# Attention and output projection in one block of the program, with values copied by ScalarE, the sums' inverses spread by TensorE, and head loops written out

## What is computed

```python
q = jnp.einsum('btc,hcd->bhtd', x, Wq) + bq[None, :, None, :]
k = jnp.einsum('btc,hcd->bhtd', x, Wk) + bk[None, :, None, :]
v = jnp.einsum('btc,hcd->bhtd', x, Wv) + bv[None, :, None, :]
scores = jnp.einsum('bhtd,bhsd->bhts', q, k) * scale
neg = jnp.finfo(scores.dtype).min
causal = jnp.triu(jnp.full((Tn, Tn), neg, dtype=scores.dtype), k=1)
probs = jax.nn.softmax(scores + causal, axis=-1)
y = jnp.einsum('bhts,bhsd->bhtd', probs, v)
y = y.transpose(0, 2, 1, 3).reshape(Bn, Tn, H * D)
return y @ Wo + bo
```

## Time and profile before

| what | us |
|---|---|
| median of 3 runs | 2577.18 (2575.45 to 2577.74) |
| profiled execution, its own time | 2575.64 |
| its span, first to last instruction | 2574.1 |
| first row product of attention | at 182.3 |
| last product of the heads ends | at 624.3 |
| first product of the output projection | at 646.9 |
| last one starts | at 698.9 |

### The profile page before, as it was taken

The page is one execution under the profiler, slowest core; times in us unless marked ns, Lnnn a source line. Parts: engine busy times, 40 slices in busy tenths (PEclk is TensorE's granted clock), DMA queues, the critical chain, the costliest instruction groups (busy, mean ns, idle before and its releaser), DMA issues. The chain is left out here.

```text
span 2574.1 us, 47582 instructions
## 1 busy us (share of the span) xinstructions
PE 2334.5 (91%) x12710; PEld 1773.7 (69%) x12712; DVE 1497.5 (58%) x3155; ACT 977.3 (38%) x2202; POOL 1094.5 (43%) x993
## 2 busy tenths in 40 slices
PE   7969998996756999999999779999989998999998
PEld 5855455443535989989989648888855664788886
DVE  6336556663566555555555457999256665655554
ACT  3114555453254444444444342222255553312221
POOL 3128888776002666666667501111166663000000
PEclk9978999998866999999999879999999999999999
DMA  5458999996355999999999834447499761000001
GB/s 178 122 175 311 346 338 329 341 326 252 116 204 145 245 283 281 258 265 273 271 263 221 149 129 148 168 163 232 141 217 225 166 151 38 13 25 25 25 9 66
DMA packets 263307, 491.18 MB, mean 191 GB/s; under 512 B 31889, under 2 KB 149137, under 8 KB 253458
## 3 DMA queue, kind: packets, MB, share of 16 engines
q1 hardware_dynamic: 197202, 272.17, 34.9%
q0 software_dynamic: 62976, 212.42, 29.4%
q10 hardware_dynamic: 3024, 5.29, 0.6%
HBM read 592.96 MB, written 198.79 MB: 308 GB/s over the span
## 5 line engine op out<-in xcount | busy, mean ns | idle before, releaser
L1431 PE MATMUL m_ps_u<-m_ring,m_xT_hi 128*128 x1280 | 370.4, 350 | 0.2 <-issue 0.2
L1399 POOL DMA_INDIRECT expert_sum<-x_res,token_of x160 | 257.1, 1607 | 182.9 <-DMA expert_sum<-x_res,token_of 66.3
L808 ACT ACTIVATE probs<-ps_c 128x512 f32<-128x512 f32 (+3 forms) x384 | 179.1, 491 | 208.7 <-PE ps_c L741 102.7
L1431 PEld LDWEIGHTS m_ps_u<-m_ring,m_xT_hi 128*128 128x128 f32 x1280 | 236.7, 190 | 1.2 <-issue 0.6
L1431 PE MATMUL m_ps_u<-m_ring,m_xT_lo 128*128 x640 | 216.9, 339 | 0.0
L1392 POOL DMA_INDIRECT m_xg<-x_rows,token_of x160 | 172.5, 1078 | 100.6 <-issue 92.3
L709 PE MATMUL ps_r<-k_st,q_st 96*128 96x512 f32 (+3 forms) x384 | 163.8, 433 | 53.4 <-DVE neg_max L838 22.4
L1878 PE MATMUL s_ps<-s_x_hi,s_w_hi 128*128 128x512 f32 x512 | 199.7, 390 | 1.6 <-POOL s_w_lo L1848 1.6
L1878 PE MATMUL s_ps<-s_x_lo,s_w_hi 128*128 128x512 f32 x512 | 199.3, 389 | 0.0
L1878 PE MATMUL s_ps<-s_x_hi,s_w_lo 128*128 128x512 f32 x512 | 199.2, 389 | 0.0
L2647 DVE TENSOR_TENSOR x_res<-f_ps_o,x_res 128x512 f32<-128x512 f32 x176 | 109.3, 684 | 143.4 <-PE f_ps_o L2540 143.4
(11 more groups left out here) (357 smaller groups left out, 5782.0 us busy)
## 6 DMA issues: line engine op xcount, KB each, us to landing
m_ring<-w_split SPq DMA_DIRECT2D x160, 1536.0 KB
m_ring<-w_split SPq DMA_DIRECT2D x160, 768.0 KB
w_split<-e_gu_parts POOLq DMA_DIRECT2D x32, 1536.0 KB
proj<-s_out SPq DMA_DIRECT2D x32, 1024.0 KB, 4.0
e_raw_gu<-w_experts POOLq DMA_DIRECT2D x32, 768.0 KB
w_split<-e_dn_parts POOLq DMA_DIRECT2D x32, 768.0 KB
e_raw_dn<-w_experts POOLq DMA_DIRECT2D x32, 512.0 KB
q_st<-q_parts SPq DMA_DIRECT2D x32, 256.0 KB
```

The source lines that it names most:

```text
L808: nc.scalar.activation(probs[a][j % RING][:, :width], ps_c[(j * BATCH + a) % BUFS][:, :width], ACT.Exp, scale=SCALE).then_inc(exp_done, 1)
L1399: pool.indirect_dma_start(acc[j % 2], rows_at(j), y[j % TURNS], None, bounds_check=PADDED - 1, oob_is_err=True, compute_op=ALU.add).then_i ...
L1431: last = nc.tensor.matmul(ps_u[b % 2][:, :W_UP], x[b % 2][:, k, :], ring[:, first + k * GU_ROW:][:, bass.ds(place, W_UP)], start=(n == 0), ...
```

## The change

- `attend` and `output_projection` are put into one block: no wait of all engines between them. The output projection's tiles come from space that the heads don't use, and GpSimd's splitting of experts may go on beside it. The split of `wo` is in two halves, each behind and ahead of GpSimd's loop.
- The loops over heads on PE, ACT, DVE and SP are written out; GpSimd keeps its loop.
- `take_v` moves from GpSimd to ACT, behind the exponentials of column 5.
- q and k lie in device memory so that a half of both batches is one piece of 4 KB per row. `q_st` has three buffers, and a whole unit's q is loaded three units ahead, at the start of a unit. `y_st` is stored in halves, each with its own semaphore.
- In `parts` three small DVE operations (add, copy, subtract) become four small reductions.
- The inverses no longer go through device memory. `of_head` holds ones where a column belongs to a head, `of_chunk` the inverses of one group with zeros elsewhere; a 32-bit product of them on PE writes the spread inverses to PSUM (`o_ps_n`), DVE multiplies y into it, and ACT and DVE take the parts from there. y has 4 buffers of one step, the spread inverses 3, the output tiles 5.

```diff
@@ attention @@
-    qk = {n: nc.dram_tensor(f"{n}_parts", (HEADS, 2, DH, N_TOK), F32).ap() for n in "qk"}
+    qk = {n: nc.dram_tensor(f"{n}_parts", (HEADS, 2, DH, 2, BATCH, GROUP), F32).ap() for n in "qk"}
...
-        attend(nc, qk, v_rows, yT, all_sums, w_raw, w_split, wo, wo_hi, wo_lo)
-        output_projection(nc, x_res, yT, all_sums, inv_sums, wo_hi, wo_lo)
+        sb = lambda n, s, dt=F32: ctx.enter_context(nc.sbuf_tensor(n, s, dt))
+        wo_hi, wo_lo = sb("wo_hi", [P, KD, D], F32R), sb("wo_lo", [P, KD, D], F32R)
...
+        sem = semaphores(ctx, nc)
+        block = ctx.enter_context(nc.Block())
+        wo_split = sem("wo_split")
+        attend(nc, block, sem, qk, v_rows, yT, all_sums, w_raw, w_split, raw, parts, wo, wo_hi, wo_lo, wo_split)
+        output_projection(nc, block, sem, x_res, ident, yT, all_sums, wo_hi, wo_lo, wo_split, in_chunk, in_head, of_head)
@@ norm_and_project, home() @@
-            return qk["qk"[m // (MT // 2)]][h0:h0 + HT, part, :, g * GROUP:(g + 1) * GROUP]
+            return qk["qk"[m // (MT // 2)]][h0:h0 + HT, part, :, g % 2, g // 2, :]
@@ attend, GpSimd @@
-            def take_v(it, e):
-                u = unit(it, e)
-                if not (isinstance(it, int) and it == 0):
-                    pool.wait_ge(pv_done, (u - 1) * PER_UNIT + BATCH * RING)
-                    pool.sem_inc(turns_begun, 1)
-                nc.gpsimd.tensor_copy(v_pair[e][:, :, :DH], v_rows[:, :, bass.ds(u * DH, DH)]).then_inc(v_ready, 1)
...
+            def split_wo(half):
+                ks = slice(half * KD // 2, (half + 1) * KD // 2)
+                pool.wait_ge(wo_loaded, half * 16 + 16)
+                pool.sem_inc(turns_begun, 1)
+                nc.gpsimd.tensor_copy(wo_hi[:, ks, :], raw_wo[:, :, :]).then_inc(wo_split, 1)
+                pool.wait_ge(wo_split, half * 2 + 1)
+                pool.sem_inc(turns_begun, 1)
+                nc.gpsimd.tensor_tensor(wo_lo[:, ks, :], raw_wo[:, :, :], wo_hi[:, ks, :].bitcast(F32), ALU.subtract).then_inc(wo_split, 1)
...
             body(0, False)
+            split_wo(0)
             with pool.Fori(1, BODIES - 1) as it:
                 body(it, False)
+            split_wo(1)
             body(BODIES - 1, True)
...
@@ attend, SP @@
...
+            def store_y(u, half):
+                sp.wait_ge(y_done, u * 2 + half + 2)
+                cols = slice(half * HALF, (half + 1) * HALF)
                 for a in range(BATCH):
-                    toks = slice(a * T, (a + 1) * T)
-                    sp.dma_start(yT[bass.ds(u, 1), :, toks].rearrange("h d t -> (h d) t"), y_st[a * COL:a * COL + DH, :]).then_inc(y_stored, 16)
-                    sp.dma_start(all_sums[bass.ds(u, 1), toks], y_st[a * COL + DH:a * COL + DH + 1, :]).then_inc(y_stored, 16)
-
-            def body(it, final):
-                for e in range(E):
-                    if not final:
-                        after_column(it, e, 3)
-                        load_q(it + 1, e, 0, low_loaded[e])
-                        after_column(it, e, 7)
-                        load_k(it + 1, e, 0, low_loaded[e])
-                        after_column(it, e, NCH - 1)
-                        load_q(it + 1, e, 1, q_up_loaded[e])
-                        load_k(it + 1, e, 1, k_up_loaded[e])
-                    store(it, e)
-
...
+                    toks = slice(a * T + half * HALF, a * T + (half + 1) * HALF)
+                    sp.dma_start(yT[u:u + 1, :, toks].rearrange("h d t -> (h d) t"), y_st[a * COL:a * COL + DH, cols]).then_inc(y_stored[half], 16)
+                    sp.dma_start(all_sums[u:u + 1, toks], y_st[a * COL + DH:a * COL + DH + 1, cols]).then_inc(y_stored[half], 16)
...
+            for u in range(HEADS):
+                if u == 1:
+                    sp.wait_ge(wo_split, 2)
+                    load_wo(1)
+                if u + E < HEADS:
+                    sp.wait_ge(cols_done, u * PER_UNIT + 8 * BATCH)
+                    load_k(u + E, 0)
+                store_y(u, 0)
+                if u + E < HEADS:
+                    sp.wait_ge(cols_done, (u + 1) * PER_UNIT)
+                    load_k(u + E, 1)
+                store_y(u, 1)
+                if u + Q_BUFS < HEADS:
+                    for half in range(2):
+                        load_q(u + Q_BUFS, half)
@@ attend, TensorE and ScalarE @@
-            body(0, True, False)
-            with pe.Fori(1, BODIES - 1) as it:
-                body(it, False, False)
-            body(BODIES - 1, False, True)
+            for it in range(BODIES):
+                body(it, it == 0, it == BODIES - 1)
...
+            def take_v(u):
+                if u >= E:
+                    act.wait_ge(pv_done, (u - 1) * PER_UNIT + BATCH * RING)
+                nc.scalar.copy(v_pair[u % E][:, :, :DH], v_rows[:, :, u * DH:(u + 1) * DH]).then_inc(v_ready, 1)
...
+                        if j == 5 and E <= unit(it, e) + 1 < HEADS:
+                            take_v(unit(it, e) + 1)
@@ attend, VectorE @@
-                    nc.vector.tensor_tensor(blocks, blocks, second[:, :, :], ALU.min).then_inc(joined, 1)
+                    nc.vector.tensor_reduce(pairs[:, :, :, 0], both_max[:, :, :, :], AX.X, ALU.min).then_inc(joined, 1)
                     dve.wait_ge(joined, u + 1)
                 if not (isinstance(it, int) and it == 0 and e == 0 and half == 0):
                     dve.wait_ge(turned, u * 2 + half)
-                nc.vector.tensor_copy(of_batch[:, :, :, 0], blocks).then_inc(parts_done, 1)
-                dve.wait_ge(parts_done, u * 4 + half * 2 + 1)
-                nc.vector.tensor_tensor(of_batch[:, :, :, 1], blocks, of_batch[:, :, :, 0].bitcast(F32), ALU.subtract).then_inc(parts_done, 1)
+                nc.vector.tensor_reduce(pairs[:, :, :, 1].bitcast(F32R), pairs[:, :, :, 0:1], AX.X, ALU.max, negate=True).then_inc(parts_done, 1)
+                nc.vector.tensor_reduce(of_batch[:, :, :, 0], pairs[:, :, :, 0:1], AX.X, ALU.max).then_inc(parts_done, 1)
+                dve.wait_ge(parts_done, u * 6 + half * 3 + 2)
+                with nc.allow_low_precision(reason="one difference, rounded once to the type that the products read"):
+                    nc.vector.tensor_reduce(of_batch[:, :, :, 1], pairs, AX.X, ALU.add).then_inc(parts_done, 1)
...
-                if half == 0:
-                    dve.wait_ge(y_stored, (u + 1) * 64)
+                dve.wait_ge(y_stored[half], (u + 1) * 64)
@@ output_projection @@
+            sp.dma_start(sums[:, :], all_sums.rearrange("h (a t) -> (h a) t", t=W_SUMS)).then_inc(sums_loaded, 16)
+            for n, (g, k) in enumerate(STEPS):
+                if n >= Y_BUFS:
+                    sp.wait_ge(y_ready, n - Y_BUFS + 1)
+                heads = yT[k * HT:(k + 1) * HT, :, g * GROUP:(g + 1) * GROUP].rearrange("h d t -> (h d) t")
+                sp.dma_start(y[n % Y_BUFS][:, :], heads).then_inc(loaded[n % Y_BUFS], 16)
...
+            def spread_inverse(n):
+                g, k = STEPS[n]
+                if n >= BUFS:
+                    pe.wait_ge(lo_done, n - BUFS + 1)
+                if k == 0:
+                    pe.wait_ge(chunk_taken, (g + 1) * PER_GROUP)
+                nc.tensor.matmul(ps_n[n % BUFS][:, :], of_head[:, k * P:(k + 1) * P], of_chunk[g % 2][:, :, :].rearrange("p c t -> p (c t)"),
+                                 start=True, stop=True).then_inc(spread, 1)
...
+            pe.wait_ge(rows_marked, 3)
+            for n in range(BUFS):
+                spread_inverse(n)
+            pe.wait_ge(wo_split, 4)
+            for n in range(len(STEPS)):
+                pe.wait_ge(lo_done, n + 1)
                 for s in range(SUB):
...
+                    project_tile(n, s)
+                if n + BUFS < len(STEPS):
+                    spread_inverse(n + BUFS)
...
+            def take_chunks(g):
+                if g >= 2:
+                    act.wait_ge(spread, (g - 1) * KD)
+                for c in range(PER_GROUP):
+                    nc.scalar.activation(of_chunk[g % 2][:, c, :], sums[:, :], ACT.Copy, scale=in_chunk[:, g * PER_GROUP + c:g * PER_GROUP + c + 1]).then_inc(chunk_taken, 1)
...
+                dve.wait_ge(loaded[n % Y_BUFS], 16 * (n // Y_BUFS + 1))
+                dve.wait_ge(spread, n + 1)
+                nc.vector.tensor_tensor(ps_n[n % BUFS][:, :], y[n % Y_BUFS][:, :], ps_n[n % BUFS][:, :], ALU.mult).then_inc(y_ready, 1)
```

More of the change, by code:

```diff
@@ L505, in attend @@
     RING = 4
+    Q_BUFS = 3
     BUFS = 3
@@ L682, in _ @@
-            sp.sem_inc(y_stored, 64)
-            for e in range(E):
-                load_q(0, e, 0, low_loaded[e])
-                load_k(0, e, 0, low_loaded[e])
-                load_q(0, e, 1, q_up_loaded[e])
-                load_k(0, e, 1, k_up_loaded[e])
-            with sp.Fori(0, BODIES - 1) as it:
-                body(it, False)
-            sp.dma_start(raw_wo[:, :, :], wo.rearrange("(k p) d -> p k d", p=P)).then_inc(wo_loaded, 16)
-            body(BODIES - 1, True)
-            sp.wait_ge(y_stored, 64 * (HEADS + 1))
```

(42 more changed lines are left out.)

178 lines of the change are left out of this document (69 added, 109 removed).

## The result

The changed kernel takes 2519.68 us (median of 4 runs, 2514.85 to 2520.5), the kernel before beside it 2577.46 (2575.45 to 2579.76): ratio 0.9772, 95% interval 0.9755 to 0.9789. The forecast was 2523. The profiled execution took 2519.35, 56.3 less than that of before.

The account below looks back on a forecast made before the run. TensorE was taken to bound the heads, with most units losing 3.3 us to waits and low clock. Units -52.6, heads to projection -4.5, projection +4.3 sum to -52.8: 2575.64 to 2523 us; own range 2513 to 2540, with rivals 2508 to 2552.

Parts of the forecast that it names:

- Units (-52.6): Heads: 14 units fall from 27.26 to 23.5 us each, 52.6 us less in all.
- late k loads: Heads: k lower, behind 0.77 MB of q in SP's queue, comes late; 0.5 us per unit, with what clock it costs.
- (c) Values on ACT: Heads: 14 value copies on ACT of about 0.6 us, mostly hidden; 0.2 us per unit, bounds 0 and 0.6.
- (d) Branches: Heads: writing the loops out brings nothing, since a branch costs nothing countable; code fetch also taken as 0.
- Between heads and projection (-4.5): From heads' end to projection's first product: 18.1 us against 22.57, 4.5 less; bounds 12 and 22.
- Projection (+4.3): Output projection: 13 spread products among its products make 56.7 us against 52.43, 4.3 more; bounds 52 and 60.
- 623 foreseen: GpSimd's experts and `wo` work end at about 623, with 24 us of cover before the projection's end at 647.
- Rivals: Faster still, 2510 (0.13); SP's queue bounds, 2554 (0.20); slower, 2613 (0.05); reductions held, 2574 to 2578 (0.02).
- SP's queue never bound: Rival for the heads: SP's queue becomes the bound, k lower late at each unit's start, 25.7 us units, 2554; chance 0.20.
- the 3.5 us that I had put beside the sum: Between heads and projection: GpSimd may hold the reciprocal of the sums, up to 3.5 us on top, giving 2525.

Follow-up runs that it names:

- e8: Changed kernel with VectorE's heads in a loop of 6 bodies again, other engines written out: median 2509.63 us, ratio to the kernel before 0.9751.
- r_after: The changed kernel measured and traced again, unedited: 2523.98 us, ratio to the kernel before 0.9788.
- e1: Changed kernel with SP's wait for the `wo` split, and the second half's load, moved from unit 1 to unit 3: 2513.3 us, ratio to before 0.9757.
- r_best: Repeat of the changed kernel with SP's `wo` wait at unit 3, second split earlier, inverses in high and low parts: 2512.70 us, ratio to before 0.9752.
- e7: Kernel before with only the small operations of `parts` turned into reductions: ratio to before 0.999.
- e10: Kernel before with only `y_st` stored in halves, each with its own semaphore, lower half's stores behind k lower: ratio to before 0.998.
- e4: Changed kernel with `attend` and `output_projection` in two blocks again: median 2592.57 us, ratio to the kernel before 1.0059.
- e6: Changed kernel with both halves of `y_st` stored together at the unit's end, and q issued ahead of k upper and the stores: ratio to before 1.0132.
- e5: Changed kernel with both halves of `y_st` stored together behind k upper, q still behind the stores: ratio to the kernel before 0.9945.

## Why the prediction was right, and where it was not

At the stage's end the sum was -52.8 and the trace has -52.6; another 3.7 came behind it, where the experts' stage was 7.1 shorter and the rest 3.4 longer, within what the experts' stage varies. The place and sign were right; the terms were less so. That the two numbers meet within 0.2 us is luck: the units gave 5.9 less than I said, the way from heads to projection 4.6 more, and unit 1's turn came 1.0 earlier, which I had left as it was.

- **Units (-52.6): measured -46.7.** From 225.15 to the heads' end at 576.52 are 351.4 us, before 398.1. Twelve units took 22.8 in the mean, at my lower bound of 22.8: ACT's copies and late k loads, for which I added 0.7, cost nothing that can be counted. But 14.9 went in unit 1 and 2 at SP's wait for `wo_split`, 9.46 of them the pause and the rest the low clock behind it. This is the step that failed: I priced what stands ahead of k lower in SP's queue in bytes and read over a wait in the same lines, with a whole unit's loads behind it. When the wait would end was to be had too: in the trace of before GpSimd's subtraction for the fifth expert, which stands behind that split now, starts at 244.6.
- **What the units' gain is due to.** I read the loss of a unit as a sum of stalls, stores and q the most, and priced the parts together. The runs show a chain. Each of four parts undone alone costs 41 to 51 of the 52.6 us at the stage's end: reductions, values and stores lengthen the units, and the one block leaves them as fast and loses their gain behind the heads. Two of the parts alone bring nothing that can be told and 0.2%. The third buffer of q, the pieces of 4 KB and the spread product in place of device memory were not taken back by themselves, so their shares stay open.
- **(c) Values on ACT: 0.2 per unit.** The price was right to within that, the meaning missed. GpSimd takes 27 us per unit, and while it copies the values, no unit can be faster for long. The number for it stood in the earlier trace rows, 27.6 us per unit beside 27.26 for PE; over all 14 traces GpSimd took 26.9 to 27.6, however fast the heads were.
- **(d) Branches: 0.** Held for DVE, the one engine tried. The rule of the Trainium skill (Runtime: NRT & Kernel Launch, Instruction fetch mechanics) is on a branch whose target lies outside the two loaded pages of 256 instructions each. A body of VectorE's loop shows 135 instructions in e8's trace, so by that rule it need not fetch, and e8 neither bears it out nor speaks against it.
- **Between heads and projection (-4.5): measured -9.1**, 13.4 us for 22.57. Stores landed by 1.2 us behind their issue where I took 4.4, the sums' load took 1.95 for 3.0, the reciprocal 1.75 for 2.75; evacuation, copies, spreads and the first parts came out within 0.3 each. The same landing took 1.2 in r_after too, but 4.0 in e1 and 3.5 in r_best, so my 4.4 lay just above what occurs, and 1.2 is at its lower end. For the kernel before I had left open what filled the time to 631.3; e7 and e10 show that GpSimd's split did.
- **Projection (+4.3): measured +4.1**, 56.52 for 56.7.
- **GpSimd.** Ended near 625 (623 foreseen), 21 us under cover. I called it cover and nothing more; e4 shows that without the one block it is the bound.
- **Rivals.** SP's queue never bound in steady units at 1.8 MB per 22.9 us, which is 79 KB per us, just above the 78 that I had worked out. What rate it could keep up was not measured: e6 has the same bytes in another order, and loses by that order.

## What to carry to other kernels

When several engines run at nearly the same pace (27.26 and 27.6 us per unit here), removing one wait may show nothing, and each one left undone may take the gain away: list every engine's and queue's own pace first, and cut all that lie above the target. Read an in-order queue for its waits as well as its bytes, and name what stands behind each. Where a background job runs beside the main one, ask what it still delivers to it: a copy, a split, the end of a block.

## What the runs showed of the hardware

- DVE's reciprocal of 128x256 took 1.752 to 1.754 us in all 14 traces, also in the six in which GpSimd computed beside it. In e1 it ran from 571.80, GpSimd's subtraction from 571.86, and neither was longer than elsewhere (in e8 GpSimd's subtraction was the first to start, and the reciprocal wasn't held either):

```profile
571.80 1.75 DVE L1018 RECIPROCAL o_sums<-o_sums 128x256 f32<-128x256 f32 x1 [7.30 <-DMA o_sums<-prob_sums]
571.86 2.34 POOL L626 TENSOR_TENSOR wo_lo<-raw_wo,wo_hi 128x1024 fp32r<-128x1024 f32 x1 [0.19 <-POOL wo_hi L623]
```

  So the 3.5 us that I had put beside the sum for it do not arise. A plain copy is held at that place: 0.43 us in e1, and in the changed kernel

```profile
577.16 3.42 POOL L589 TENSOR_TENSOR e_gu_parts<-e_raw_gu,e_gu_parts 128x1536 fp32r<-128x1536 f32 x1 [0.18 <-POOL e_gu_parts L586]
...
577.76 3.10 DVE L1016 COPY o_of_head<-o_in_head 128x512 f32<-128x512 f32 x1
```

  which ends 0.28 us behind GpSimd's operation. The Trainium skill (SBUF — State Buffer, Who interferes with whom) says so of copies and of operations with two SBUF inputs, and that a reduction never contends; the traces agree, with 174 ns at most for the small reductions. That section does not name the reciprocal.
- The issue of a small store on SP's queue took 0.31 us in the median, but 0.9 us or more in 14 of 128 in the changed kernel (1.54 at most) and in 34 of 128 in e5 (1.70 at most). Eight in a row do not make it by themselves: e6 issues them so too and has 11 of 128. What does was not found.
